# Slots of the side work dealt anew in a chunked state-space scan

## The reference, cut to what matters

```python
u, res = jnp.split(x @ W_in, 2, axis=-1)
u = silu(conv3(u))
dt, Bm, Cm = jnp.split(u @ W_x, [RANK, RANK + 16], axis=-1)
delta = softplus(dt @ W_dt + b_dt)
deltaA = exp(delta * A);  deltaB_u = (delta * u) * Bm
h = deltaA * h + deltaB_u          # scan over the tokens, for 16 states
y = sum over the states of h * C
y = (y + u * D_param) * silu(res)
x = layernorm(x + y @ W_out)
logits = x @ router_w.T
```

## Time and profile before

| | us |
|---|---|
| median of three runs | 2743.27 |
| the profiled execution | 2720.49 |
| its span | 2718.7 |
| TensorE busy | 2395.2 (88%) |
| VectorE busy | 2138.2 (79%) |
| GpSimd busy | 1801.6 (66%) |
| ScalarE busy | 1757.7 (65%) |
| mean granted TensorE clock | 0.954 |

### The profile page before, as it was taken

The page is one execution under the profiler, slowest core; times in us unless marked ns, Lnnn a source line. Parts: engine busy times, 40 slices in busy tenths (PEclk is TensorE's granted clock), DMA queues, the critical chain, the costliest instruction groups (busy, mean ns, idle before and its releaser), DMA issues. The chain is left out here.

```text
span 2718.7 us, 44389 instructions
## 1 busy us (share of the span) xinstructions
PE 2395.2 (88%) x14152; PEld 1856.4 (68%) x14152; DVE 2138.2 (79%) x2860; ACT 1757.7 (65%) x2991; POOL 1801.6 (66%) x877
## 2 busy tenths in 40 slices
PE   7899999998998998999999997644999999999991
PEld 2466756666666666666666675544899989989991
DVE  0599989988988999998999999957566567557644
ACT  3688878887887887887878888632244334334434
POOL 0787977987888888788788789722155336425524
PEclk9899999999999999999999999975999999999996
DMA  2111211111121112121111112111031322323116
GB/s 69 39 48 55 71 56 61 66 56 56 63 66 54 63 56 67 60 63 57 62 56 63 63 48 71 55 63 49 25 79 34 80 60 44 76 62 78 34 20 253
DMA packets 84403, 169.87 MB, mean 62 GB/s; under 512 B 8480, under 2 KB 52000, under 8 KB 84144
## 3 DMA queue, kind: packets, MB, share of 16 engines
q1 hardware_dynamic: 68784, 145.72, 15.9%
q0 software_dynamic: 15360, 20.98, 4.6%
HBM read 130.49 MB, written 36.18 MB: 61 GB/s over the span
## 5 line engine op out<-in xcount | busy, mean ns | idle before, releaser
L387 POOL TENSOR_TENSOR dbu<-du,b_all 128x2048 f32<-128x2048 f32 x256 | 1161.2, 4543 | 159.3 <-DVE hst L599 159.2
L467 ACT ACTIVATE da<-delta,a_neg 128x512 f32<-128x512 f32 x1008 | 689.3, 691 | 132.4 <-DVE hst L599 118.0
L599 DVE TENSOR_TENSOR_SCAN hst<-da,dbu 128x512 f32<-128x512 f32 x504 | 592.5, 1212 | 110.2 <-ACT da L467 108.3
L599 DVE TENSOR_TENSOR_SCAN hst<-da,carry,dbu 128x512 f32<-128x512 f32 x504 | 621.1, 1271 | 39.9 <-ACT da L467 33.7
L1500 PE MATMUL gu<-x_part,w_part 128*128 128x384 f32 (+1 forms) x2304 | 485.6, 360 | 5.3 <-POOL w_part L1227 2.1
L697 PEld LDWEIGHTS hd<-ident,hst 128*128 128x128 f32 x2048 | 238.5, 142 | 328.1 <-DVE yacc L554 156.8
L697 PE MATMUL hd<-ident,hst 128*128 128x128 f32 x2048 | 323.5, 281 | 124.2 <-DVE yacc L554 105.6
L1500 PEld LDWEIGHTS gu<-x_part,w_part 128*128 128x128 f32 x2304 | 403.5, 189 | 35.5 <-issue 4.4
L554 DVE SCALAR_TENSOR_TENSOR yacc<-hd,c_tok,yacc 128x512 f32<-128x512 f32 x512 | 375.9, 734 | 52.3 <-PE hd L697 47.2
L634 PE MATMUL gen<-xT,w_u 128*128 128x512 f32 x768 | 390.2, 602 | 13.9 <-DVE w_u L539 12.5
L454 ACT ACTIVATE hTC<-w,c_tok 128x512 f32<-128x512 f32 x512 | 347.5, 679 | 58.4 <-PE w L697 57.7
(11 more groups left out here) (205 smaller groups left out, 2928.0 us busy)
## 6 DMA issues: line engine op xcount, KB each, us to landing
b_all<-b_rows SPq DMA_DIRECT2D x128, 512.0 KB, 3.7
xT<-in_xT SPq DMA_DIRECT2D x16, 514.0 KB, 4.9
x_rows<-in_x SPq DMA_DIRECT2D x16, 512.0 KB, 3.9
x_dram<-x SPq DMA_DIRECT2D x16, 512.0 KB, 3.1
acc_dram<-x SPq DMA_DIRECT2D x16, 512.0 KB, 4.5
w_raw<-in_wg SPq DMA_DIRECT2D x8, 1024.0 KB, 5.0
w_raw<-in_wu SPq DMA_DIRECT2D x8, 1024.0 KB, 8.0
w_raw<-in_wd SPq DMA_DIRECT2D x8, 1024.0 KB, 12.7
```

Source lines behind the costliest of these rows:

```text
L387: nc.gpsimd.tensor_tensor(dbu[DBU[n]][:], du[parity][:], b_n, ALU.mult).then_inc(dbu_ready, 1)
L467: nc.scalar.activation(da_bank[t % 2][:], delta[parity][:, t, :], ACT.Exp, scale=a_neg[:, t, n:n + 1]).then_inc(da_ready, 1)
L599: nc.vector.tensor_tensor_scan(hst[DBU[n]][:, t, :], decay[:], dbu[DBU[n]][:, t, :], initial, ALU.mult, ALU.add).then_inc(scanned, 1)
```

## The change

The slots of most fills and reads are dealt anew, nine fills are put ahead of the transposition of their slot, and some of the other slots and states move. The order in which fills get full, which `nth_full` counts, now puts a fill ahead of another of the same last slot if it is in `BEFORE_TURN`. The wait of a logarithm pass names its exponential pass through `SOFT_ORDER`; the number is the same as before.

```diff
-EARLY_SLOT, EARLY_AT, EARLY_BANK, EARLY_STATE = 20, 17, 1, 4
+EARLY_SLOT, EARLY_AT, EARLY_BANK, EARLY_STATE = 20, 16, 1, 4
...
-FILL_AT = {"r0": (0, 0, 1), "r1": (1, 2, 3), "C0": (0, 4), "C1": (1, 6), "r2": (0, 9, 10), "r3": (1, 11, 12),
-           "o0": (0, 14, 15, 16, 17), "o1": (1, 21, 21, 21, 22, 22), "xd": (0, 22, 23, 24, 25),
-           "u0": (1, 25, 26, 27, 29, 30, 30), "cT": (0, 28), "d0": (0, 31), "d1": (1, 33), "d2": (0, 35),
-           "d3": (1, 37), "u1": (0, 40, 41, 42, 43, 44, 45), "u2": (1, 46, 47, 48, 49, 50, 51), "ud0": (0, 48),
-           "xt0": (0, 51), "xt1": (0, 54), "u3": (1, 54, 55, 56, 57, 58, 59), "ud1": (0, 57), "lg": (0, 60)}
-READ_AT = {"r0": 4, "r1": 6, "C0": 7, "C1": 9, "r2": 13, "r3": 15, "o1": 24, "xd": 27, "cT": 30, "u0": 32,
-           "d0": 33, "d1": 35, "d2": 38, "d3": 40, "u1": 47, "ud0": 50, "u2": 53, "xt0": 53, "xt1": 56, "ud1": 59,
-           "u3": 61, "lg": 62}
-BEFORE_TURN = ()
+FILL_AT = {"r0": (0, 1, 1), "r1": (1, 1, 3), "C0": (0, 4), "C1": (1, 5), "r2": (0, 8, 8), "r3": (1, 10, 12),
+           "o0": (0, 14, 17, 19, 19), "o1": (1, 21, 21, 22, 22, 23), "xd": (0, 23, 25, 25, 25), "cT": (0, 27),
+           "u0": (1, 28, 30, 30, 32, 32, 32), "d0": (0, 30), "d1": (1, 33), "d2": (0, 35),
+           "u1": (1, 37, 39, 40, 40, 41, 42), "d3": (0, 39), "ud0": (0, 45), "u2": (1, 46, 46, 47, 48, 50, 50),
+           "xt0": (0, 49), "xt1": (1, 53), "ud1": (0, 54), "u3": (1, 55, 55, 58, 58, 59, 61), "lg": (1, 62)}
+READ_AT = {"r0": 4, "r1": 5, "C0": 5, "C1": 11, "r2": 14, "r3": 16, "o1": 25, "xd": 27, "cT": 30, "u0": 34, "d0": 31,
+           "d1": 36, "d2": 38, "d3": 40, "u1": 45, "ud0": 48, "u2": 53, "xt0": 53, "xt1": 54, "ud1": 55, "u3": 61,
+           "lg": 63}
+BEFORE_TURN = ('C0', 'd0', 'd3', 'lg', 'o1', 'r0', 'u3', 'ud0', 'ud1')
...
-SEED_AT, ACC_READ_AT = (8, 10), (7, 9)
-SILU_AT, STATS_AT, EXP_AT, LN_AT, NORM_AT = 19, 25, (41, 42), (43, 44), (45, 46, 48, 49)
-GATE_AT, SMALL_AT, ADD_AT, DU_AT = {5: 1, 6: 0}, 11, 14, 15
+SEED_AT, ACC_READ_AT = (7, 10), (7, 8)
+SILU_AT, STATS_AT, EXP_AT, LN_AT, NORM_AT = 19, 26, (43, 46), (49, 50), (41, 44, 45, 46)
+GATE_AT, SMALL_AT, ADD_AT, DU_AT = {4: 1, 6: 0}, 9, 15, 15
+SOFT_ORDER = sorted(EXP_AT + LN_AT)
...
-        return self.base() + sorted(self.fills, key=lambda x: FILL_AT[x][-1]).index(name)
+        return self.base() + sorted(self.fills, key=lambda x: (FILL_AT[x][-1], x not in BEFORE_TURN)).index(name)
...
-                        act.wait_ge(soft_step, c * 4 + (5 + h))
+                        act.wait_ge(soft_step, c * 4 + (5 + SOFT_ORDER.index(EXP_AT[h])))
```

## The result

The changed kernel takes 2700.34 us (median of four runs, 2697.74 to 2702.71), the kernel before, beside it, 2744.47. The ratio is 0.9837, with a 95% interval of 0.9820 to 0.9855. The same kernel gave 0.9826 (0.9812 to 0.9839) in a later group of runs (e8). Forecast were 2698 us in a range of 2672 to 2738: it holds.

A forecast was written before the change was run, and what follows sets the result against it. With all four engines over 80% busy, the order of the work was taken to decide. Terms of 21 + 9 + 0 + 15 - 2 + 2 = 45 us off the median 2743.3 gave 2698, range 2672 to 2738.

The forecast's parts named there:

- slots 20 to 37: Term for chunks 1 to 13: `o1` ahead of slot 21's transposition uses TensorE's idle time; 13 x 1.6 = 21 us.
- low clock at slot 21: Term: filling the idle time there ends six of seven 1.5 us spells at clock 0.50; 9 us gained.
- slots 37 to 51: Term: ScalarE decides here and its work fits the same room; 0, bounds 0.5 us a chunk either way.
- slots 51 to 63: Term: TensorE's crowding goes, 1.7 us even, 1.0 odd; GpSimd's late products cost even chunks 0.3; 15 us gained.
- start: Ahead of chunk 0: reads of `u1` and `ud0` between the passes end the last some 4.5 us later; loss 2 us.
- chunk 0: Term: chunk 0 has the same tail as the later chunks; gain 2 us.
- rest: Chunks 14 and 15, which lack most fills, and the moves within slots 1 to 16: nothing.
- The walk: Stepping chunk 8 through the new slots without semaphore gaps; it put slot 37's addition at 1003.2, 2.4 us earlier.
- The price of slot 21: Its transposition behind two parts makes its addition 0.2 us late; costed at nothing, as VectorE waits for ScalarE's decay anyway.
- TensorE's work is the bound: Rival, chance 0.10: slots 20 to 37 keep their length, as their set of fills is the same; 2719 us.
- The low clock moves: Rival, chance 0.08: 1.5 us spells come at slots 15, 16 and 18 in 14 chunks, costing 21; 2728 us.
- The softplus chain: Rival, chance 0.12: reads between the passes delay the last pass, slot 60 waits 3.3 to 4.0 us; slower, 2761 us.

The follow-up runs named there:

- e8: The changed kernel again, with no edit, in a later group of runs; 2699.72 us, ratio 0.9826 to the kernel before.
- e2: The kernel before with only `o1` put ahead of the transposition of slot 21; 2703.88 us, ratio 0.9953 to the kernel before.
- e3: The kernel before with only the last two parts of `o0` moved to slot 19; 2710.71 us, ratio 0.9971 to the kernel before.
- e11: e7 with the last two normalisations two slots later (47 and 48, not 45 and 46); 2693.82 us, ratio 0.9795 to the kernel before.
- e6: The changed kernel with fills and reads from `u2` on in their old slots, four fewer names in `BEFORE_TURN`; 2732.27 us, ratio 0.9949 to the kernel before.
- e5: The changed kernel with the softplus passes, normalisations and delta's addition in their old places; 2697.94 us, ratio 0.9818 to the kernel before.
- e7: The changed kernel with, ahead of chunk 0, `u0` to `u3` in alternate banks and passes at slots 41 to 44; 2691.99 us, ratio 0.9800.
- e10: e7 with the reads of `d0`, `u0` and `d1` and the fill of `d1` one slot later; 2678.41 us, ratio 0.9866 to the kernel before.
- e4: The changed kernel with every fill behind its transposition (`BEFORE_TURN` empty); 2759.74 us, ratio 1.0164 to the kernel before.

## Why the prediction was right, and where it was not

It came out 2 us off. The terms missed by more, in both directions, and measured profile against profile they don't come to 45 us but to 54.5, while the medians of the runs gave 44. So the closeness of the sum is in part luck. The profile before has the longest scan stage of the three, with the most starts at the low clock, and against the other two the gain is 48 to 51.

| term | forecast | measured, profile against profile |
|---|---|---|
| slots 20 to 37 | 21 | 30.0, less 3.4 on the way to the mark: 26.6 |
| low clock at slot 21 | 9 | 10.8 (7 starts; with 4 or 6 of them 6.5 or 9.4) |
| slots 37 to 51 | 0 | 0 |
| slots 51 to 63 | 15 | 12.5 |
| start | -2 | -7.6 |
| chunk 0 | +2 | +4.2 |
| rest (chunks 14 and 15, slots 1 to 5, the turn) | 0 | 8.3 |

- **Slots 20 to 37.** The idle time was filled, as the step said, and the part of `xd` is out of the way. The walk had given 2.4 us a chunk; measured are 2.39 in even and 2.24 in odd chunks behind the mark, and 2.1 and 2.0 from the addition of slot 19. I had gone halfway down to the sure 0.7 for want of trust in it. The walk's remaining wait, for the decay behind the read of `u0`, was put at 1.6 us; there are two, of 0.66 and 1.08, behind the reads of `d0` and `u0`, which waited 0.72 and 2.03. The price of slot 21 was put at nothing behind ScalarE's cover: the way to the mark is 0.24 us a chunk longer, and 1.1 in e2, where slot 19 has no fill. (In even chunks 0.22 of the 0.24 come in e3 too, from `o0` in slot 19 alone.) Without that step of the change some 0.9 us a chunk more would have gone there.
- **Low clock.** All seven starts are gone. e3 has none left and e2 one, so that either of the two moves does nearly all of it. But the step said that idle time is filled; e3 gets there with the idle time only moved and parted.
- **Slots 37 to 51.** Zero was right in its number, and e11 supports its reason: in ScalarE's full stretch the amount of its work decides. But e6 shows a limit to it: with the fills of before, the passes' new places cost 1.0 us. The fills must have been moved with them.
- **Slots 51 to 63.** The two terms have about their size along one way of the square of e5 and e6, and not along the other. GpSimd's price was too small: the four operations and two carries end 18.9 us behind slot 47 (993.22 to 1012.15) and not 18.4, so that the wait is 0.68 and not 0.3. Hence 18.09 in even chunks and not under 17.8. This wait was named as a sign of being wrong, though the sum itself had 0.3 of it; the sign came, and the sum held.
- **The start** is the mis-sized term. I counted two reads between the passes as 4.5 us of delay; the last pass ends ten later, at 82.06. Before, ScalarE's passes began at 68.00, and TensorE's `xd` at 47.98:
```profile
68.00 2.00 ACT L505 ACTIVATE tmp<-tmp 128x1024 f32<-128x1024 f32 x2
```
```profile
47.98 6.42 PE L642 MATMUL gen<-u,w_x 128*48 128x512 f32 x8 [4.00 <-ACT u L496]
```
  After, ScalarE's timeline:
```profile
72.28 1.06 ACT L506 ACTIVATE tmp<-tmp 128x1024 f32<-128x1024 f32 x1
78.15 0.60 ACT L410 ACTIVATE u_raw<-gen 128x512 f32<-128x512 f32 x1 [4.81 <-PE gen L635]
78.64 1.05 ACT L506 ACTIVATE tmp<-tmp 128x1024 f32<-128x1024 f32 x1
```
  and TensorE's:
```profile
51.10 5.30 PE L643 MATMUL gen<-u,w_x 128*48 128x512 f32 x8 [4.00 <-ACT u L497]
...
70.88 7.23 PE L635 MATMUL gen<-xT,w_u 128*128 128x512 f32 x10
```
  The read waits 4.81 us for the last five parts of `u1`, with nothing beside them (a part of `u` is one matmul, two records, and not two matmuls). They take 7.23 us, most of it in a spell at 0.50 (the mean clock from 70.9 to 78.1 is 0.63); five parts of `u` just ahead, at 60.27, take 4.56. And `u1` went from bank 0 to bank 1, which I had not weighed at all: in the first stage all four `u` now share a bank, each fill waits for the read of the one ahead, `xd` starts 3.1 us later, and the first pass 4.3. e5 returns the first of the two, e7 both.
- **Chunk 0** gained 4.2 us and not 2, and not in its tail: slots 51 to 63 take 18.0 us as before. Before, the additions of slots 11 and 13 waited 1.68 and 0.93 us for transpositions, which is gone (2.8 us in slots 5 to 19), and slots 37 to 51 are 1.2 shorter.
- **The rest.** Chunks 14 and 15 gave 2.6 us, slots 1 to 5 gave 4.8 and the turn 0.9. The 4.8 go with the low clock again: at the loop's five turns a spell at 0.50 begins in four in the profile before and in two in the profile after, and the odd chunk behind such a turn takes 0.9 to 2.8 us too long to its slot 5. Over all profiles it is one to five of the five, in every version, so that the change isn't shown to have a part in it.

The rivals. *TensorE's work is the bound* was wrong for this step, but holds in the state that it leaves: 39 us without a pause, and e10. *The low clock moves* did not happen in chunks 1 to 13: the pauses in slots 15 to 18 are there (0.49 and 0.77 us in chunk 8) and the granted clock stays at 1.00 there. By the Trainium skill ("TensorE: Matmul & The Clock Gate", HAM oscillation) short bursts between waits send the array back again and again; these did not (in the page's example the waits are longer). It does happen in e10, though, at another place and behind a shorter pause than those, and behind the loop's turns. *The softplus chain*: in the loop neither `u1` nor `ud0` makes ScalarE wait, and the last pass begins at 996.38, 3.2 us behind slot 47, and ends at 4.2 as walked. Ahead of chunk 0 just this happened, where no scans give the fills their lead. What I had not as a rival is e4: without the nine names in `BEFORE_TURN` chunks 1 to 13 take 1419.2 us and not 1334.4, more than the whole gain. I had them at nothing, except `o1`, and named only the waits that they could bring. Where a read is put one slot behind its fill, the order within the slot is a term.

## What to carry to other kernels

Where several engines follow one order written by hand, slots, order within a slot and the places of the reads are one thing. Together they gained 44 us here. The new slots without the new order lost 42 against the kernel before (e4), the old slots from `u2` on gave up 33 of the gain (e6), three reads a slot later lost 14 (e10), and the order of `o1` or the slots of `o0` alone gained only 13 and 7 (e2, e3). Look at the ramp-up apart from the loop: a schedule that is right in the steady state lost 7.6 us there, and a few lines that treat it for itself brought the first scan back to within 1 us (88.91 and 88.23 against 88.33). And before trusting a difference of one per cent between two profiles, compare a stage that neither kernel changes.

## What the runs showed of the hardware

- The low clock (0.50 granted, 1.2 GHz) at slot 21 came in 7, 6 and 4 of 13 chunks of the same code, behind pauses of 0.55 and 1.12 us in even and 1.23 and 1.18 in odd chunks, and cost 1.5 to 1.7 us each. In the eleven profiles of other versions it came there once (e2, chunk 1). In e3 pauses of nearly the same sum (0.71 and 0.93, 1.23 and 0.93), with 4.0 us of work between them and not 0.7, brought it in none of 13. In e10 it came in 4 of 13 chunks at slots 35 to 41, behind one pause of 0.47 us in a stretch otherwise without any, and lasted 3 to 7 us; in the changed kernel pauses of 0.49 and 0.77 us at slots 15 to 18 brought it in none of chunks 1 to 13. So the length of a pause alone does not tell; what does is open.
- Behind the loop's turn, where TensorE stands still for 2.3 to 3.5 us, the low clock came at one to five of the five turns, in all 14 profiles, and cost up to 3.0 us each.
- The same expert code takes 745 or some 775 us: 745 to 747 on chips 12 and 14, 771 to 780 on chips 11 and 5. Of the 31.7 us between the two profiles 18.9 are TensorE busy (733.77 against 752.65 us from the first to the last gate-and-up matmul, at a granted clock of 1.00 and 0.98), the others pauses. The clock alone doesn't tell the two apart: it is 0.99 in this stage in e4 (747 us) and in e6 (771 us). What differs on the chips is open.
- At the loop's turn ScalarE stands still for 1.7 to 3.5 us and TensorE for 2.3 to 3.5, ended by nothing that the profile shows ("issue"). Where the tail was 0.5 to 0.6 us faster (e5, e11), the step across the turn was 0.4 to 0.9 longer. This is ScalarE in e5; 2.63 stand there after the change:
```profile
1014.82 1.30 ACT L468 ACTIVATE da<-delta,a_neg 128x512 f32<-128x512 f32 x2 [3.05 <-issue]
```
